# A fused perceiver, attention and expert block: way back and small scores side by side, keys and values in other PSUM banks

## The chip, the cores and the metric

The kernel runs on one NeuronCore of a Trainium2 chip. The metric is the device time of one execution, in microseconds. The engines are TensorE (PE), VectorE (DVE), ScalarE (ACT), GpSimd (POOL) and SyncE (SP, which issues the transfers here). Each takes its instructions in the order in which the program gives them, and semaphores tie the engines to each other.

## What is computed

The input is x, 64 sequences of 32 tokens with 256 features, and a context of 257 rows of 192 features for each sequence. Three residual blocks follow each other, each behind a layer norm:

```python
x = x + xattn(layernorm(x), context)   # top-32 cross attention, FiLM, state-space layer, FFN
x = x + attn(layernorm(x))             # softmax attention, 256 wide within 32 tokens
x = x + ffn(layernorm(x))              # 8 experts, top 2 by router and centroids
```

In xattn, four heads of queries score the 257 context rows, keep 32 each, and their mean weights give a context vector c_t. From it come scale and shift ahead of a state-space layer (the film's input half), and scale and shift behind it (the output half): `y = s4d(x_in); y = y * (1 + g * scale_out) + g * shift_out; xt = x_text + y`. Then come a layer norm, a GELU network of 1024, and another norm. The state-space layer is a convolution over 32 tokens, here as a transform of real matrices: a matmul forward, a product with the kernel's transform, and a matmul back ("the way back"). In attn, `scores = Q @ K.T / 4`, `out = softmax(scores) @ V`, followed by an output projection. In ffn each expert is `gelu(x @ w1 + b1) @ w2 + b2`, summed with the gates. Everything is in float32.

## The kernel before

The 2048 tokens are 16 tiles of 128 rows (four sequences each). The kernel is a software pipeline of four stages: in step n (n = 1 to 18) each engine works for tile a = n (cross attention: scores and top 32), b = n - 1 (context, film, state-space layer, first network), c = n - 2 (its end, then small attention) and dd = n - 3 (experts). A tile out of 0 to 15 is None and its work is left out, so a is None from step 16, and dd is there from step 3. `following` is a's next tile. Every engine's part of a step is a hand-written order in its function `step`; semaphores count what is done, and `wait(engine, semaphore, value)` stands ahead of the instruction that needs it.

PSUM has eight banks of 512 columns: S[0], S[1] (scores of a), B0, B1, PA, C0, D0, D1. An expert's output k goes to half a bank, to D1 for k = 0, 1, 4, 5 and to D0 for k = 2, 3, 6, 7.

The part of a step that the change touches, on PE in its order (L numbers are the lines of the kernel before):

- scores_end(a, 1): the last matmuls of a's scores (L1187, L1190).
- experts 0 and 1 of dd (L1257), into D1.
- The way back of b (L1355): for each of four sequences a matmul of 96 contracted rows to 32 output rows, 256 columns, into B0's upper half. It waits for both halves of had (L970, L973 on DVE) and for `qk_a`, the copies of the folded queries.
- transposes of xl2 of c (L1145) into C0's lower half.
- The film's output half of b (L1362, L1363): 512 columns into B1.
- Keys of c (L1368, the product of query and key weights with xT2) into C0's upper half, values (L1370) into C0's lower half. They wait for xT2_a.
- experts 2 and 3 (L1257), into D0, behind g2b_a, the experts' second gelu.
- Small scores of c (L1380): eight matmuls to 32 output rows and 32 columns, into C0.
- query of the tile after following (L1152), into PA's upper half.
- experts 4 to 7 (L1257). Experts 4 wait until DVE has taken outputs 0 and 1 (`acc_v`), experts 6 until it has taken 2 and 3.
- The output of small attention (L1406), 32 matmuls, behind pT_blk; transposes of hn (L1145); expert bias (L1255); output projection (L1417); the first network (L1240), and in the next step its second half (L1263).

On ACT: gelus of dd (L634, helper `gelus`), the copies of the folded queries (L650, `keyed`), exps(a, 1) (L671, two Exp), copy of xT2 (L629, helper `copy`, as all copies with a semaphore), of the way back's result to yb (L629, semaphore y_a), of keys (L720) and values (L629, v_a), Exp of the small scores (p_c, L723), copy of the query. A table load (ACT_TABLE_LOAD) stands wherever the next function is in another table.

On DVE: maxima and take (L810, L817) of a's second half, gated(0, 1) (L883, L885: takes expert outputs out of PSUM times their gates), take8 (L837), then y times scale and plus shift (L986, L989), xt (L995), its statistics (L1000, L1001) with a find8 (L831, maximum search) between them, gated 2 (L889), the row maximum of the small scores (L1008), gated 3 (L889), the row weights of the softmax (L1013 to L1015), hn (L1018, behind POOL's root `rs0_g`), pT_blk (L1021), gated 4 and 5. The softmax weights pT_blk are the transposed weights spread over four blocks.

## Time and profile before

| | us |
|---|---|
| median of 3 runs | 589.39 (585.61 to 591.86) |
| the profiled execution | 583.03 |
| its span, first to last instruction | 581.2 |
| PE, DVE busy in it | 540.8, 481.4 |
| ACT, POOL busy in it | 295.5, 287.3 |

The profile is one execution. A row of a timeline gives the start in us from the span's start, the time from the first start to the last end, engine, line, operation, what is written from what, the shape, and how many. In brackets stands idle time before it, and what ended it. PEld is the loading of weights. Most matmuls in float32 appear as two records. The names are those of buffers: PC is PA and C0, BB is B0 and B1, D is D0 and D1, and ang is the large buffer that most of the small tiles share.

### The profile page before, as it was taken

The numbers are of one execution on the slowest core, as the hardware profiler recorded it, in microseconds if no ns is written. First come the engines' busy times: TensorE is split into PE (matmuls) and PEld (weight loads), VectorE is DVE, ScalarE is ACT, GpSimd is POOL, SyncE is SP. The second block draws the span as 40 slices with busy tenths as digits, with TensorE's granted clock in tenths as the row PEclk, the third lists the DMA queues.
The fourth block names the chain that finished last, engine by engine and source line by source line (L and its number), as shares of the span: only waits on it lengthen the run. The fifth ranks groups of instructions, "written<-read, shape, count | busy, mean of one in ns | idle before, by whom it ended". The sixth has DMA issues, their size and how long they took to land.

```text
span 581.2 us, 13157 instructions
## 1 busy us (share of the span) xinstructions
PE 540.8 (93%) x4580; PEld 401.6 (69%) x4580; DVE 481.4 (83%) x1748; ACT 295.5 (51%) x770; POOL 287.3 (49%) x669
## 2 busy tenths in 40 slices
PE   2868878999999999999999999999999999998986
PEld 1425454868686877778686868687877868685854
DVE  7898786789998989889898989898988989885444
ACT  3131443374746555564737474746555564645533
POOL 5972155626445375636363635546272636262521
PEclk9998988999999999999999999999999999999999
DMA  8972412030403040220303040404030120000000
GB/s 190 339 293 99 197 42 83 2 117 2 136 1 136 1 124 13 68 70 21 114 20 117 3 135 0 136 1 134 3 114 23 54 73 11 1 11 1 11 1 18
DMA packets 17957, 42.33 MB, mean 73 GB/s; under 512 B 2770, under 2 KB 9570, under 8 KB 17380
## 3 DMA queue, kind: packets, MB, share of 16 engines
q1 hardware_dynamic: 17892, 41.51, 21.3%
q8 instruction: 36, 0.59, 0.4%
q14 instruction: 29, 0.24, 0.1%
HBM read 39.37 MB, written 2.13 MB: 71 GB/s over the span
## 4 chain that ended last, share of the span: by engine, by line
PE 80%; DVE 10%; POOL 2%; issue 2%; ACT 2%; DMA 1%; SPq 1%; DVEq 0%; ACTq 0%; POOLq 0%
PE D L1240 10%; PE BB L1240 9%; PE BB L1263 9%; PE D L1257 8%; PE SS L1181 5%; PE SS L1187 3%; PE BB L1228 3%; PE BB L1229 3%; PE PC L1417 2%; PE BB L1363 2%; PE BB L1362 2%; PE PC L1368 2%; PE PC L1213 2%; PE PC L1370 2%; PE PC L1406 2%
## 5 line engine op out<-in xcount | busy, mean ns | idle before, releaser
L551 POOL TENSOR_SCALAR var_in<-mv 128x1 f32<-128x1 f32 x64 | 14.5, 226 | 203.8 <-DVE mv L1001 116.1
L837 DVE MATCH_REPLACE8 work<-top,work 128x257 f32<-128x257 f32 x192 | 77.6, 410 | 0.0
L831 DVE MAX8 top<-work 128x8 f32<-128x257 f32 x192 | 73.1, 415 | 0.0
L1240 PE MATMUL D<-ang,e_w 128*128 128x128 f32 x512 | 69.7, 281 | 0.0
L1240 PEld LDWEIGHTS D<-ang,e_w 128*128 128x128 f32 x512 | 61.6, 192 | 10.0 <-issue 10.0
L1257 PE MATMUL D<-expw,ang 128*128 128x256 f32 x256 | 65.7, 389 | 1.8 <-ACT ang L634 1.8
L1240 PEld LDWEIGHTS BB<-ang,w 128*128 128x128 f32 x512 | 59.6, 192 | 1.9 <-ACT ang L734 1.1
L1240 PE MATMUL BB<-ang,w 128*128 128x128 f32 x512 | 59.9, 276 | 0.9 <-ACT ang L734 0.9
L634 ACT ACTIVATE ang<-BB,cols 128x128 f32<-128x128 f32 x128 | 36.5, 368 | 47.0 <-PE BB L1240 47.0
L1263 PE MATMUL BB<-expw,ang 128*128 128x256 f32 x256 | 57.9, 380 | 0.0
L1257 PEld LDWEIGHTS D<-expw,ang 128*128 128x128 f32 x256 | 45.8, 190 | 12.9 <-issue 4.5
L1263 PEld LDWEIGHTS BB<-expw,ang 128*128 128x128 f32 x256 | 47.5, 191 | 5.7
L889 DVE SCALAR_TENSOR_TENSOR ang<-D,gate,ang 128x256 f32<-128x256 f32 x96 | 43.1, 477 | 6.0 <-PE D L1257 4.1
L671 ACT ACTIVATE expo<-SS,nmax,srs 128x257 f32<-128x257 f32 x64 | 32.7, 561 | 18.2 <-DVE work L817 17.8
L1181 PE MATMUL SS<-ctx_t,qk 128*128 128x257 f32 x128 | 35.5, 402 | 3.9 <-DMA mask_t<-mask_scratch 2.7
L553 POOL TENSOR_TENSOR rstd<-var_in,mhalf 128x1 f32<-128x1 f32 x64 | 36.5, 570 | 5.3
L671 ACT ACT_TABLE_LOAD x28 | 35.9, 1283 | 0.5
L634 ACT ACTIVATE ang<-D,cols 128x128 f32<-128x128 f32 x128 | 35.7, 355 | 0.2
L1181 PEld LDWEIGHTS SS<-ctx_t,qk 128*128 128x128 f32 x128 | 23.5, 202 | 12.8 <-issue 9.5
L584 POOL TENSOR_SCALAR wsel<-head,rsum_row,tm_tile 128x32 f32<-128x32 f32 x64 | 29.4, 471 | 3.8 <-issue 1.2
L629 ACT ACTIVATE ang<-D 128x256 f32<-128x256 f32 x16 | 6.1, 383 | 43.3 <-PE D L1145 43.3
L810 DVE MAX8 top<-SS 128x8 f32<-128x257 f32 x64 | 24.2, 418 | 4.2 <-PE SS L1190 4.2
(279 smaller groups left out, 1253.4 us busy)
## 6 DMA issues: line engine op xcount, KB each, us to landing
ctx_n<-in_ctx_n SPq DMA_DIRECT2D x16, 768.0 KB, 4.4
ctx_t<-in_ctxT SPq DMA_DIRECT2D x16, 514.0 KB
ctx_t<-in_ctxT SPq DMA_DIRECT2D x16, 257.0 KB
xT<-in_xT SPq DMA_DIRECT2D x16, 128.0 KB, 2.8
x_all<-in_x SPq DMA_DIRECT2D x4, 512.0 KB, 11.3
out<-out_sb SPq DMA_DIRECT2D x16, 128.0 KB, 1.7
ctx_l<-in_ctx_l SPq DMA_DIRECT2D x16, 96.0 KB, 5.1
w<-in_W SPq DMA_DIRECT2D x1, 1024.0 KB
```

What stands on the lines that cost most here:

```text
L553: link(tt(rstd[k][:, 0:1], w, mhalf[:, 0:1], ALU.pow))
L584: nc.gpsimd.tensor_scalar(wsel[:, k, :], sel[:, :], rsum_row[:, k:k + 1], tm_tile[:, k:k + 1], ALU.mult, ALU.mult).then_inc(s["wsel_g"], 1)
L634: ins = A(dst[:, k, :], bank[:, 128 * (k % 4):128 * (k % 4) + 128], ACT.Gelu, bias=bias[:, k:k + 1])
L671: A(expo[:, 2 * q + k, :], S[k][:, 0:G], ACT.Exp, bias=nmax[:, 2 * q + k:2 * q + k + 1], scale=srs[:, a.n, 2 * q + k:2 * q + k + 1]).then_ ...
L810: V.max(top[:, 2 * q + k, 0:8], S[k][:, 0:G]).then_inc(chains["top"], 1)
L831: V.max(top[:, 2 * q + k, 8 * r8:8 * r8 + 8], work[:, 2 * q + k, :]).then_inc(chains["top"], 1)
L837: V.match_replace(work[:, 2 * q + k, :], top[:, 2 * q + k, 8 * r8:8 * r8 + 8], work[:, 2 * q + k, :], TAKEN).then_inc(chains["taken"], 1)
L889: V.scalar_tensor_tensor(acc[k % 2][:, :], bank, gate[:, k:k + 1], acc[k % 2][:, :], ALU.mult, ALU.add).then_inc(s["acc_v"], 1)
L1181: MM(S[u][:, 0:G], qk1[a.p][:, 2 * q + u, :, :].rearrange("p h t -> p (h t)"), ctx_t1[a.p][:, 2 * q + u, :], start=True, stop=False)
L1240: ins = MM(bank[:, 128 * m:128 * m + 128], w[:, k, at:at + 128], xs[:, 128 * k:128 * k + 128], start=k == 0, stop=k == 1)
L1257: MM(bank, act2[:, k, :], e_w2[:, k, :], start=True, stop=True).then_inc(s["eo_mm"], 1)
L1263: ins = MM(B1[:, 0:D], act1[:, k, :], w2[:, k, :], start=k == 0, stop=k == HID // 128 - 1)
```

## The change

It holds in steps where tiles b and dd both exist (`joined(b, dd)`, steps 3 to 16). Elsewhere the old order stays.

PE: the transposes of xl2 go ahead of experts 0 and 1 and into D0, with a wait for g2b_a. After experts 0 and 1 come the keys (into D0's upper half), the film's output half, the way back, the small scores (into C0 as before), the values (now into PA's lower half), experts 2 and 3, and the query, which has a new wait until the values are copied.

ACT: the copy of xT2 and of the keys go ahead of exps(a, 1), each from D0, the keys behind a semaphore of their own (key_mm); the copy of the values goes behind the Exp of the small scores and comes from PA.

DVE: both find8 and the row maximum go ahead of the y multiply; the row weights go ahead of gated 2; pT_blk goes behind gated 3 and ahead of hn.

The diff, cut to its core (the helper functions repeat the old instructions):

```diff
+        def joined(b, dd):
+
+            return bool(b and dd)
...
+            def columns(c, bank):
+
+                wait(act, s["xT2_mm"], c.count(1, 1))
+                copy(xT2[:, :], bank[:, 0:D], "xT2_a")
+
+            def keys(c, bank):
+
+                wait(act, s["key_mm"], c.count(1, 1))
+                copy(xmT[:, :], bank[:, D:2 * D], "v_a")
+
+            def values(c, bank):
+
+                wait(act, s["v_mm"], c.count(1, 1))
+                copy(v_c[:, :], bank[:, 0:D], "v_a")
...
...
                     gelus(act2, 1, D0, e_b1, "e1b_mm", "g2b_a", dd)
                 if following:
                     keyed(following)
+                if joined(b, dd):
+                    columns(c, D0)
+                    keys(c, D0)
                 if a:
                     exps(a, 1)
-                if c:
-                    wait(act, s["xT2_mm"], one(c))
-                    copy(xT2[:, :], C0[:, 0:D], "xT2_a")
+                if c and not joined(b, dd):
+                    columns(c, C0)
                 if c and c.n == NT - 1:
                     A(ahead[:, :], b1[:, 0:1], ACT.Exp)
                 if b:
                     wait(act, s["inv_mm"], one(b))
                     copy(yb[:, :], B0[:, D:2 * D], "y_a")
-                if c:
+                if c and not joined(b, dd):
                     wait(act, s["v_mm"], one(c))
-                    A(xmT[:, :], C0[:, D:2 * D], ACT.Copy)
-                    copy(v_c[:, :], C0[:, 0:D], "v_a")
+                    keys(c, C0)
+                    values(c, C0)
+                if c:
                     wait(act, s["nmaxc_v"], one(c))
                     A(p_c[:, :], C0[:, D:D + T], ACT.Exp, bias=nmax_c[:, :], accum_out=sum_c[:, :]).then_inc(s["pc_a"], 1)
+                if joined(b, dd):
+                    values(c, PA)
                 if next_tile(following):
                     query(next_tile(following))
...
+            def row_maximum(c):
+
+                wait(dve, s["s_mm"], c.count(1, 1))
+                V.reduce_max(nmax_c[:, :], C0[:, D:D + T], AXX, negate=True).then_inc(s["nmaxc_v"], 1)
+
+            def row_weights(c):
+
+                wait(dve, s["pc_a"], c.count(1, 1))
+                link(V.reciprocal(rsum_c[:, :], sum_c[:, :]))
+                link(V.tensor_scalar(pn_c[:, :], p_c[:, :], rsum_c[:, :], None, ALU.mult))
+                V.transpose(pT_c[:, :], pn_c[:, :]).then_inc(chains["pT"], 1)
+
+            def weight_blocks(c):
+
+                wait(dve, chains["pT"], c.count(1, 1))
+                V.tensor_tensor(pT_blk[:, :, :], pT_c[:, :].rearrange("p (o t) -> p o t", o=1).broadcast_to([128, BT, T]), block_mask[:, :, :], ALU.mult).then_inc(s["pt_v"], 1)
...
...
                     gated(range(0, 2))
                 if a:
                     take8(a, 0, 2, (1,))
+                if joined(b, dd):
+                    if a:
+                        find8(a, 0, 3)
+                    row_maximum(c)
                 if b:
                     wait(dve, s["y_a"], one(b))
                     wait(dve, s["y_mm"], one(b))
...
                 if b:
                     wait(dve, chains["y"], b.count(2, 1))
                     V.tensor_tensor(yb[:, :], yb[:, :], B1[:, D:2 * D], ALU.add).then_inc(chains["y"], 1)
-                if a:
...
-                if a:
+                if a and not joined(b, dd):
...
...
                     V.bn_aggr(mv[0][:, :], bn[0][:, :]).then_inc(s["st0_v"], 1)
                 if a and a.n == 1:
                     tokens(4, 8)
+                if joined(b, dd):
+                    row_weights(c)
                 if dd:
                     gated((2,))
-                if c:
-                    wait(dve, s["s_mm"], one(c))
-                    V.reduce_max(nmax_c[:, :], C0[:, D:D + T], AXX, negate=True).then_inc(s["nmaxc_v"], 1)
+                if c and not joined(b, dd):
+                    row_maximum(c)
                 if dd:
                     gated((3,))
                 if c:
-                    wait(dve, s["pc_a"], one(c))
-                    link(V.reciprocal(rsum_c[:, :], sum_c[:, :]))
-                    link(V.tensor_scalar(pn_c[:, :], p_c[:, :], rsum_c[:, :], None, ALU.mult))
-                    V.transpose(pT_c[:, :], pn_c[:, :]).then_inc(chains["pT"], 1)
+                    if joined(b, dd):
+                        weight_blocks(c)
+                    else:
+                        row_weights(c)
                 if b:
                     wait(dve, s["rs0_g"], one(b))
                     V.tensor_scalar(hn[:, :], xt[:, :], mv[0][:, 0:1], rstd[0][:, 0:1], ALU.subtract, ALU.mult).then_inc(s["hn_v"], 1)
-                if c:
-                    wait(dve, chains["pT"], one(c))
-                    V.tensor_tensor(pT_blk[:, :, :], pT_c[:, :].rearrange("p (o t) -> p o t", o=1).broadcast_to([128, BT, T]), block_mask[:, :, :], ALU.mult).then_inc(s["pt_v"], 1)
+                if c and not joined(b, dd):
+                    weight_blocks(c)
                 if dd:
...
+                def film_out():
+
+                    MM(B1[:, :], zT1[:, :], film1[:, 512:1024], start=True, stop=False)
+                    MM(B1[:, :], zT2[:, :], film2[:, 512:1024], start=False, stop=True).then_inc(s["y_mm"], 1)
...
+                def keys_values(keys, values):
+
+                    wait(pe, s["xT2_a"], one(c))
+                    if keys is not None:
+                        for m in range(2):
+                            for k in range(2):
+                                ins = MM(keys[:, D + 128 * m:D + 128 * m + 128], qk_w[:, k, 128 * m:128 * m + 128], xT2[:, 128 * k:128 * k + 128], start=k == 0, stop=k == 1)
+                        ins.then_inc(s["key_mm"], 1)
+                    if values is not None:
+                        for k in range(2):
+                            ins = MM(values[:, 0:D], xT2[:, 128 * k:128 * k + 128], wv_w[:, k, :], start=k == 0, stop=k == 1)
+                        ins.then_inc(s["v_mm"], 1)
+
+                def small_scores():
+
+                    wait(pe, s["v_a"], c.count(2, 1 if joined(b, dd) else 2))
+                    wait(pe, s["x2_v"], c.count(1, 0))
+                    for k in range(BT):
+                        rows = slice(T * k, T * k + T)
+                        for m in range(2):
+                            cols = slice(128 * m + T * k, 128 * m + T * k + T)
+                            ins = MM(C0[rows, D:D + T], xmT[:, cols], xT2[:, cols], start=m == 0, stop=m == 1)
+                    ins.then_inc(s["s_mm"], 1)
...
                     scores(a, 1)
                 if a:
                     scores_end(a, 1)
+                if joined(b, dd):
+                    wait(pe, s["xl2_v"], one(c))
+                    wait(pe, s["g2b_a"], one(dd))
+                    if dd.n == 0:
+                        pe.wait_ge(s["route_a"], 1)
+                    transposes(D0, xl2, "xT2_mm")
                 if dd:
                     experts(range(0, 2))
-                if b:
-
-                    wait(pe, s["had_v"], b.count(2, 2))
-                    if following:
-                        wait(pe, s["qk_a"], following.count(2, 2))
-                    if b.n == 0:
-                        pe.wait_ge(s["ld_w"], LD_W)
-                    for k in range(BT):
-                        ins = MM(B0[T * k:T * k + T, D:2 * D], dft_y[:, :], had[0:NF, k, :], start=True, stop=True)
-                    ins.then_inc(s["inv_mm"], 1)
-                if c:
-                    wait(pe, s["xl2_v"], one(c))
-                    wait(pe, s["x2_v"], c.count(1, 0))
-                    transposes(C0, xl2, "xT2_mm")
-                if b:
-                    MM(B1[:, :], zT1[:, :], film1[:, 512:1024], start=True, stop=False)
-                    MM(B1[:, :], zT2[:, :], film2[:, 512:1024], start=False, stop=True).then_inc(s["y_mm"], 1)
-                if c:
-                    wait(pe, s["xT2_a"], one(c))
-                    for m in range(2):
-                        for k in range(2):
-                            ins = MM(C0[:, D + 128 * m:D + 128 * m + 128], qk_w[:, k, 128 * m:128 * m + 128], xT2[:, 128 * k:128 * k + 128], start=k == 0, stop=k == 1)
-                    for k in range(2):
-                        ins = MM(C0[:, 0:D], xT2[:, 128 * k:128 * k + 128], wv_w[:, k, :], start=k == 0, stop=k == 1)
-                    ins.then_inc(s["v_mm"], 1)
+                if joined(b, dd):
+                    keys_values(D0, None)
+                    free_banks()
+                    film_out()
+                    way_back()
+                    small_scores()
+                    keys_values(None, PA)
+                elif b:
+                    free_banks()
+                    way_back()
+                    if c:
+                        columns(C0)
+                    film_out()
+                elif c:
+                    columns(C0)
+                if c and not joined(b, dd):
+                    keys_values(C0, C0)
                 if dd:
                     experts(range(2, 4))
-                if c:
-                    wait(pe, s["v_a"], one(c))
-                    for k in range(BT):
-                        rows = slice(T * k, T * k + T)
-                        for m in range(2):
-                            cols = slice(128 * m + T * k, 128 * m + T * k + T)
-                            ins = MM(C0[rows, D:D + T], xmT[:, cols], xT2[:, cols], start=m == 0, stop=m == 1)
-                    ins.then_inc(s["s_mm"], 1)
+                if c and not joined(b, dd):
+                    small_scores()
                 if next_tile(following):
                     if dd:
                         wait(pe, s["gT_a"], one(dd))
+                    if joined(b, dd):
+                        wait(pe, s["v_a"], c.count(2, 2))
                     query(next_tile(following))
                 if a and a.n == 1:
                     wait(pe, s["mr1_v"], following.count(4, 0))
...
                 if c:
 
                     wait(pe, s["pt_v"], one(c))
+                    wait(pe, s["v_a"], c.count(2, 2))
```

## Rows read from the trace of the kernel before

**Rows 1.** The page's totals by engine: busy us, share of the span, instructions.

```profile
PE 540.8 (93%) x4580; PEld 401.6 (69%) x4580; DVE 481.4 (83%) x1748; ACT 295.5 (51%) x770; POOL 287.3 (49%) x669
```

**Rows 2.** Busy us (instructions) of PE, PEld, DVE, ACT, POOL; clock, DMA, GB/s; L1406 one step earlier.

```profile
311.00:342.00 31.00, 30.99 (x277) 23.75 (x273) 27.40 (x105) 17.82 (x47) 15.47 (x37) 1.00 0.18 59
...
290.23 0.65 PE L1406 MATMUL PC<-ang,pT_blk 128*32 128x64 f32 x32
```

**Rows 3.** PE in order of time, one step: start us, us, what, out<-in, shape.

```profile
312.34 1.13 PE L1257 MATMUL D<-expw,ang 128*128 128x256 f32 x4
313.40 0.64 PE L1355 MATMUL BB<-had,dft_y 96*32 96x256 f32 x8
313.97 0.44 PE L1145 MATMUL PC<-head,ang 128*128 128x128 f32 x2
314.24 1.02 PE L1362 MATMUL BB<-film,zT 128*128 128x512 f32 x2
...
315.96 1.05 PE L1368 MATMUL PC<-ang,qk_w 128*128 128x128 f32 x8
316.86 1.03 PE L1370 MATMUL PC<-wvo,ang 128*128 128x256 f32 x4
317.72 1.03 PE L1257 MATMUL D<-expw,ang 128*128 128x256 f32 x4
318.68 0.35 PE L1380 MATMUL PC<-ang 128*32 128x32 f32 x16
318.96 0.71 PE L1152 MATMUL PC<-xT,head 128*128 128x128 f32 x4
319.51 1.89 PE L1257 MATMUL D<-expw,ang 128*128 128x256 f32 x8
321.41 0.65 PE L1406 MATMUL PC<-ang,pT_blk 128*32 128x64 f32 x32
```

**Rows 4.** ACT in order of time, the same step; in brackets idle time before.

```profile
309.82 1.09 ACT L634 ACTIVATE ang<-D,cols 128x128 f32<-128x128 f32 x4
...
312.56 0.55 ACT L650 ACTIVATE qk<-BB 128x256 f32<-128x256 f32 x2 [0.24 <-DVE had L970]
313.13 1.28 ACT L671 ACT_TABLE_LOAD   x1
...
315.61 0.39 ACT L629 ACTIVATE ang<-BB 128x256 f32<-128x256 f32 x1
...
319.40 0.29 ACT L723 ACTIVATE p_c<-PC,nmax_c 128x32 f32<-128x32 f32 x1 [0.82 <-DVE nmax_c L1008]
```

**Rows 5.** DVE in order of time, the same step.

```profile
315.56 0.41 DVE L837 MATCH_REPLACE8 work<-top,work 128x257 f32<-128x257 f32 x1
316.24 0.42 DVE L986 TENSOR_TENSOR ang<-ang,BB 128x256 f32<-128x256 f32 x1 [0.26 <-PE BB L1363]
...
317.69 0.42 DVE L831 MAX8 top<-work 128x8 f32<-128x257 f32 x1
318.03 0.41 DVE L1000 BATCH_NORM_STATS2 bn<-ang 128x6 f32<-128x256 f32 x1
318.47 0.18 DVE L1001 BATCH_NORM_AGGREGATE mv<-bn 128x2 f32<-128x6 f32 x1
...
319.19 0.18 DVE L1008 TENSOR_REDUCE nmax_c<-PC 128x1 f32<-128x32 f32 x1
319.29 0.48 DVE L889 SCALAR_TENSOR_TENSOR ang<-D,gate,ang 128x256 f32<-128x256 f32 x1
319.81 0.16 DVE L1013 RECIPROCAL rsum_c<-sum_c 128x1 f32<-128x1 f32 x1
...
320.74 0.41 DVE L1018 TENSOR_SCALAR ang<-ang,mv,rstd 128x256 f32<-128x256 f32 x1 [0.21 <-POOL rstd L413]
321.07 0.28 DVE L1021 TENSOR_TENSOR pT_blk<-pT_c,cols 128x128 f32<-128x128 f32 x1
```

**Rows 6.** ACT in step 16, the table load ahead of p_c.

```profile
534.95 1.28 ACT L723 ACT_TABLE_LOAD   x1
```

More of the change, by code:

```diff
@@ L717, in step @@
                     copy(yb[:, :], B0[:, D:2 * D], "y_a")
+                if c and not joined(b, dd):
+                    wait(act, s["v_mm"], one(c))
+                    keys(c, C0)
+                    values(c, C0)
                 if c:
[L719 to L721 removed]
                     wait(act, s["nmaxc_v"], one(c))
                     A(p_c[:, :], C0[:, D:D + T], ACT.Exp, bias=nmax_c[:, :], accum_out=sum_c[:, :]).then_inc(s["pc_a"], 1)
+                if joined(b, dd):
+                    values(c, PA)
                 if next_tile(following):
@@ L995, in step @@
                     V.tensor_tensor(xt[:, :], yb[:, :], xln[b.n % 3][:, :], ALU.add).then_inc(s["xt_v"], 1)
-                if a:
+                if a and not joined(b, dd):
                     find8(a, 0, 3, (1,))
@@ L1257, in experts, with free_banks, way_back, columns @@
                             MM(bank, act2[:, k, :], e_w2[:, k, :], start=True, stop=True).then_inc(s["eo_mm"], 1)
+                def free_banks():
+                    wait(pe, s["had_v"], b.count(2, 2))
+                    if following:
+                        wait(pe, s["qk_a"], following.count(2, 2))
+                def way_back():
+                    if b.n == 0:
+                        pe.wait_ge(s["ld_w"], LD_W)
+                    for k in range(BT):
+                        ins = MM(B0[T * k:T * k + T, D:2 * D], dft_y[:, :], had[0:NF, k, :], start=True, stop=True)
+                    ins.then_inc(s["inv_mm"], 1)
+                def film_out():
+                    MM(B1[:, :], zT1[:, :], film1[:, 512:1024], start=True, stop=False)
+                    MM(B1[:, :], zT2[:, :], film2[:, 512:1024], start=False, stop=True).then_inc(s["y_mm"], 1)
+                def columns(bank):
+                    wait(pe, s["xl2_v"], one(c))
+                    wait(pe, s["x2_v"], c.count(1, 0))
+                    transposes(bank, xl2, "xT2_mm")
+                def keys_values(keys, values):
[11 more added lines that the diff above has]
+                    wait(pe, s["v_a"], c.count(2, 1 if joined(b, dd) else 2))
+                    wait(pe, s["x2_v"], c.count(1, 0))
+                    for k in range(BT):
+                        rows = slice(T * k, T * k + T)
[3 more added lines that the diff above has]
+                    ins.then_inc(s["s_mm"], 1)
                 def down(half):
```

4 lines of the change are left out of this document (2 added, 2 removed).

## The prediction

> **What bounds the kernel now.** I read the totals by engine first: TensorE (PE) is busy for 93% of the span, VectorE (DVE) for 83%, ScalarE (ACT) for half [rows 1]. An average of that sort hides the stages, so the table by stretches came next: in a stretch of 31 us in the middle PE is busy for 30.99 us at granted clock 1.00 and DVE for 27.40 [rows 2]. One step of the pipeline takes 31.18 us (two starts of L1406, 290.23 and 321.41) [rows 2, 3]. I therefore follow one step, from 312.3 to 322 us, in order of time on each engine.
>
> PE goes from block to block without a gap. A block's price is the distance to the next block's start [rows 3]: experts 0 and 1 1.06 us, the way back 0.57, the transposes of xl2 0.27, the film's output half 1.72 (two weights), keys 0.90, values 0.86, experts 2 and 3 0.96, small scores 0.28, query 0.55, experts 4 to 7 1.90. Some are dearer than their streaming. Two query matmuls with 128 columns are a quarter of the film's streaming (0.43), but cost 0.55 behind the small scores; experts 2 and 3 cost 0.10 more than the values, which are of the same shape. The extra stands where 32-column blocks (way back, small scores) meet full ones.
>
> The second thing to see is how near DVE is. It waits 0.26 us for the film's output (L986), and from there it works almost without pause to pT_blk, ready at 321.07 + 0.28 = 321.35 [rows 5]. L1406, which waits for pT_blk, starts at 321.41 [rows 3]. PE and DVE are both late there to within some 0.1 us. ACT has room: its y copy (L629, 315.61) is done at 316.00 [rows 4], before DVE takes it.
>
> **The change part by part.** It holds for steps that have b and dd, n = 3 to 16: 13 with tile a (3 to 15), and step 16 without.
>
> *PE's order.* New: transposes (to D0), experts 0 and 1, keys (to D0), film, way back, small scores, values (to PA), experts 2 and 3, query, experts 4 to 7. No matmul is added or dropped. Two 32-column blocks with full ones around each become one, so one of two entries and one of two exits goes. Bare streaming of the blocks from 312.34 to 319.51, by the film's 1.72 for 1024 columns, is 3584 columns (experts 1024, film 1024, keys 512, values 512, query 256, the way back's four parallel outputs as 256) or 6.02 us, with 0.22 for the transposes and about 0.2 for the small scores 6.4; the blocks take 7.17 [rows 3]. Of the 0.7 left over at most about half goes (0.35); adding block by block with the extras where full and 32-column blocks still meet gives 0.16. I take 0.3. Below nothing it can't go, since the new order has fewer changes of width. Experts 4 would start at 319.2.
>
> *Wait for g2b_a ahead of the transposes.* D0 is still read by the second gelus, which end at 309.82 + 1.09 = 310.91 [rows 4]; PE is there at 312.34. Nothing, with 1.4 us of cover.
>
> *Keys, and ACT behind them.* This is where I expect the price. ACT takes instructions in order, and its copies of xT2 and keys now stand ahead of the exponentials exps(a, 1). ACT ends keyed at 312.56 + 0.55 = 313.11 and copies xT2 till 313.51 (0.38 us a copy). PE: transposes from 312.34, experts 0 and 1 till about 313.5, keys from 313.6, whose last result is there 1.05 later [rows 3], at 314.65. ACT stands idle from 313.51, copies the keys till 315.05, and only then runs the table load for Exp, which ran at 313.13 before. Nor can the load be hoisted: in step 16 it stands at 534.95, behind two copies, with Exp's use after it, though ACT had been idle [rows 6]. From the load's start to the y copy's end it was 316.00 - 313.13 = 2.87 [rows 4]; now y_a comes at 315.07 + 2.87 - 0.27 (the xT2 copy that stood between is gone) = 317.7, which is 1.7 later than before.
>
> At this place a rule can be weighed. The rows show the load at 1.28 us and the next Exp work at once behind it, in 2.87 for the load, two exponentials and two copies [rows 4]. The Trainium skill (ScalarE: Activation LUTs, "What ACT_TABLE_LOAD costs") puts a drain of about 1.38 us on top of the load. By that y_a would be 1.38 later still and the whole some 18 us dearer; the rows of this case have no room for it, and I give it no chance of its own.
>
> *DVE.* It ends L837 at 315.97, fills 0.75 with two maxima (0.42 each, overlapping), and then waits for the small scores [rows 5]. PE: film from 314.5 to 316.2, way back to about 316.75, small scores to 316.95, last result (0.35 after their start) at about 317.15. Row maximum 317.2 to 317.38. Then y waits for y_a till 317.73. What follows has no filler left: multiply, add, xt, bn_stats, bn_aggr at the 0.44 that L1000 to L1001 shows for a dependent pair, so aggr starts at 317.73 + 4 x 0.44 = 319.49 and ends at 319.67 (before: 318.65). Row weights (three operations, L1013 to L1015) take 320.74 - 0.21 - 319.81 = 0.72 and now stand ahead of gated 2 and 3. They run from 319.60 (an operation starts some 0.08 before the one before has ended) to 320.3; their input p_c needs 0.41 from row maximum or y copy [rows 4, 5], so it is there at 318.1. Gated 2 and 3 take 0.40 + 0.48: from 320.24 to 321.12 (before: 319.77).
>
> *The wait that takes the place.* Experts 6 and 7 write D0, where 2 and 3 stand, and so wait for acc_v of gated 3. PE arrives there at 319.2 + 0.87 = 320.1 and waits till 321.17 (0.05 behind DVE, as at L1406): 1.1 us. Queued behind are L1406 and the rest of the step. Experts 6 and 7 with the entry to 32 columns take 0.96: L1406 starts at 322.13, against 321.41. **+0.72 us a step.** PE's 0.3 saved only lengthens this wait. pT_blk comes at 321.4, no longer late: the wait that the change could take away is worth at most 0.1.
>
> *After it.* The normalization's root on POOL stays 320.74 - 318.65 = 2.09 long, so hn starts at 321.8 and is ready at 322.2, before the transposes at 322.7. DVE comes out 0.8 later, PE 0.72, and everything to the step's end follows PE as before.
>
> *Values to PA, and query's wait for them.* PE ends values at about 317.9, ACT copies them by 318.5; PE, with experts 2 and 3 between, reaches the query at 318.8. Nothing, with 0.3 of cover. Without the cover it would only eat into the 1.1 of the wait behind.
>
> *Step 16.* There is no a, so ACT has no exponentials. The load for p_c (534.95) runs over a microsecond earlier, since the value copies no longer stand ahead of it, while y comes later, behind film and way back, by about 0.6. Experts 6 and 7 have the same new wait. One against the other, between -1 and +0.7 us once; I take nothing [rows 6].
>
> **The sum.** 13 x 0.72 = 9.4 us. On the profiled execution, 583.03 us with a span of 581.2, that is 592.4. That execution is 1.1% below the median of the runs shown, 589.39; on the median it gives 598.8.
>
> **Rivals.**
> - *y is not late.* If the exponentials' work got out of y's way (a table load that overlaps the wait for the keys), y would follow the row maximum at 317.38, 0.35 earlier: +0.37 a step, +4.8 us, 594.2. For it: ACT idles 1.1 us ahead of the keys. Against: rows 6. Chance 0.17.
> - *DVE is in time (not slower).* Should the dependent chain run so tight that gated 3 ends by 320.05, PE's saving comes through: 0.3 and the 0.1 at L1406, 13 x 0.4 = 5.2 us, 584.2. The point is 320.1 at experts 6; DVE would have to be 1.1 us faster than worked out. For it: PE is the busiest engine, and L1406 really waits on DVE. Against: even with y at once behind the row maximum gated 3 ends at 320.8. Chance 0.1.
> - *DVE carries its delay on.* DVE leaves the place 0.1 later than PE; if links cost 0.3 more in the row weights and y (no filler between them), the wait grows to 1.4, +1.02 a step, +13.3 us, 602.7. For it: five dependent operations now stand bare. Chance 0.13.
> - My forecast: 0.6.
>
> **Numbers.** A measurement of this kernel tells about 1% from no change. Slower by over 1% (above 595.3): my case nearly whole, the carried delay, part of the first rival: 0.69. Within 1%: most of the first rival and much of the second: 0.23. Faster by over 1%: 0.08, if the second gives a little more than worked out. The range takes the first rival and the third, with about 2 us to the side for the spread of runs: 588 to 604.
>
> **What the profile would show.** Right: L1257 for experts 6 and 7 with PE idle 0.8 to 1.3 us before it, released by DVE L889; ACT idle about 1.1 us before the key copy and the table load some 1.9 us later in the step; DVE idle about 0.5 before the row maximum and 0.35 before the y multiply; 31.9 us from one L1406 to the next. Wrong: no idle time before experts 6, or a period at or below 31.18, or the table load standing ahead of the key copy.

## The result and the profile after

The changed kernel takes 599.39 us (median of 4 runs, 596.42 to 601.25), against 588.21 us for the kernel before (4 runs, 585.61 to 591.86). The ratio is 1.0205, with a 95% interval of 1.0148 to 1.0261: the change is slower, by 1.5 to 2.6%, and whether by more than 2% these runs don't tell. The forecast was 598.8. Some executions of these kernels run longer at a lower granted clock, and the ratios in this document leave them out.

The profiled execution took 598.03 us, with a span of 596.2 us. Its totals by engine (they answer to [rows 1]):

```profile
PE 545.3 (91%) x4580; PEld 402.9 (68%) x4580; DVE 481.7 (81%) x1748; ACT 296.6 (50%) x770; POOL 287.8 (48%) x669
```

No engine works noticeably more than before: PE 545.3 us against 540.8, DVE 481.7 against 481.4. What grew is the time in which PE has nothing to do. The span is 15.0 us longer than that of the kernel before, and the starts of the small attention's output (L1406, now L1495) divide it. Over the 13 steps 3 to 15 its start moves by 417.77 us (104.37 to 522.14), against 406.55 (101.42 to 507.97): **11.2 us, 0.86 a step**. The period of a step in the middle is 32.06 us against 31.18. Steps 16 and 17 give 0.1, the tail 0.7, and 2.95 lie ahead of step 3, where nothing was changed. The stretch from 50 to 60 us shows what goes with it (table by stretches, columns as in [rows 2]), first for the kernel before:

```profile
50.00:60.00 10.00, 8.73 (x177) 5.62 (x177) 7.62 (x19) 1.23 (x4) 0.00 (x0) 0.87 0.55 202
```

and for the changed kernel:

```profile
50.00:60.00 10.00, 9.54 (x126) 5.12 (x130) 7.28 (x19) 0.28 (x1) 0.00 (x0) 0.53 0.57 215
```

The granted clock of this stretch is 0.87 of full speed in one and 0.53 in the other. That is not the work of the change, since ahead of step 3 nothing differs: in the profiles of the ten kernels below it lies between 0.50 (three) and 1.00 (four), and the latter reach the first output some 5 us or more before the former. From here on I compare periods of a step. In each profile but those of e4 and e10 they repeat within 0.02 us from 260 to 480 us (in e4 within 0.05, and one period of e10 is 0.06 shorter). One earlier step, from about 230 us on, takes some 0.9 us more in every kernel, the one before included.

PE in one step after the change, in order of time, columns as in [rows 3]:

```profile
320.58 0.44 PE L1190 MATMUL D<-head,ang 128*128 128x128 f32 x2
...
324.50 0.64 PE L1315 MATMUL BB<-had,dft_y 96*32 96x256 f32 x8
324.96 0.34 PE L1350 MATMUL PC<-ang 128*32 128x32 f32 x16
325.23 1.13 PE L1339 MATMUL PC<-wvo,ang 128*128 128x256 f32 x4
...
327.50 1.03 PE L1302 MATMUL D<-expw,ang 128*128 128x256 f32 x4
329.31 1.13 PE L1302 MATMUL D<-expw,ang 128*128 128x256 f32 x4 [0.77 <-DVE ang L930]
330.37 0.65 PE L1495 MATMUL PC<-ang,pT_blk 128*32 128x64 f32 x32
330.95 0.44 PE L1190 MATMUL BB<-head,ang 128*128 128x128 f32 x2
331.32 0.70 PE L1300 MATMUL D<-e_b,gateT 128*128 128x256 f32 x2
331.86 1.03 PE L1506 MATMUL PC<-wvo,ang 128*128 128x256 f32 x4
```

The step's first block starts at 320.58 where it was 312.34, so 8.24 is to be taken off to compare with [rows 3]. Up to experts 4 PE needs 6.92 us (320.58 to 327.50), against 7.17 (312.34 to 319.51): the new order does save 0.25. The way back takes 0.46 until the small scores start, and these 0.27; ahead of the way back the film's second half costs 0.95 (323.55 to 324.50), where it was 0.86 (315.10 to 315.96). Then experts 6 and 7 (L1302 at 329.31) wait for DVE's L930, gated 3. From experts 4 to L1495 it is 2.87 us instead of 1.90. A second loss stands behind it: from L1495 to the output projection (L1506) it is 1.49 instead of 1.32, since the transposes are followed by the bias expert only after 0.37, not 0.28, and this by the projection after 0.54, not 0.46. From there to the next step's start, 20.78 against 20.79, nothing differs. Three terms and this rest so make the period: 6.92 + 2.87 + 1.49 + 20.78 = 32.06.

ACT in the same step, answering to [rows 4]:

```profile
321.25 0.39 ACT L633 ACTIVATE ang<-D 128x256 f32<-128x256 f32 x1
322.89 0.38 ACT L633 ACTIVATE ang<-D 128x256 f32<-128x256 f32 x1 [1.25 <-PE D L1335]
323.29 1.28 ACT L690 ACT_TABLE_LOAD   x1
324.58 1.02 ACT L690 ACTIVATE expo<-SS,nmax,srs 128x257 f32<-128x257 f32 x2
325.50 0.38 ACT L633 ACTIVATE ang<-BB 128x256 f32<-128x256 f32 x1
```

The xT2 copy at 321.25, 1.25 us of waiting for the keys, their copy, and only then the table load at 323.29. The y copy ends at 325.88, or 317.64 on the old clock; it was 316.00.

DVE, answering to [rows 5]:

```profile
325.38 0.19 DVE L891 TENSOR_REDUCE nmax_c<-PC 128x1 f32<-128x32 f32 x1 [0.50 <-PE PC L1350]
325.91 0.42 DVE L1031 TENSOR_TENSOR ang<-ang,BB 128x256 f32<-128x256 f32 x1 [0.34 <-ACT ang L633]
...
327.74 0.18 DVE L1046 BATCH_NORM_AGGREGATE mv<-bn 128x2 f32<-128x6 f32 x1
327.84 0.13 DVE L896 RECIPROCAL rsum_c<-sum_c 128x1 f32<-128x1 f32 x1
...
328.42 0.83 DVE L930 SCALAR_TENSOR_TENSOR ang<-D,gate,ang 128x256 f32<-128x256 f32 x2
329.17 0.28 DVE L903 TENSOR_TENSOR pT_blk<-pT_c,cols 128x128 f32<-128x128 f32 x1
330.07 0.41 DVE L1064 TENSOR_SCALAR ang<-ang,mv,rstd 128x256 f32<-128x256 f32 x1 [0.62 <-POOL rstd L417]
330.40 0.87 DVE L930 SCALAR_TENSOR_TENSOR ang<-D,gate,ang 128x256 f32<-128x256 f32 x2
```

It waits 0.50 for the small scores and 0.34 for y's copy, then works without fillers to the end of gated 3 (329.25), on which experts 6 start 0.06 later. hn waits 0.62 for POOL's root, and gated 4 and 5 behind it end at 331.27; the bias expert starts at 331.32.

### The profile page after: what moved, and what is told of

Its sections match the earlier page's. It is cut to its first block, busy times and chain, and to the rows that moved or that the text cites. A ratio compares the mean times of both kernels' runs of the same rounds, so it can differ in the third digit from the quotient of the medians.

```text
span 596.2 us, 13190 instructions
## 1 busy us (share of the span) xinstructions
PE 545.3 (91%) x4580; PEld 402.9 (68%) x4580; DVE 481.7 (81%) x1748; ACT 296.6 (50%) x770; POOL 287.8 (48%) x669
## 3 DMA queue, kind: packets, MB, share of 16 engines
HBM read 39.37 MB, written 2.13 MB: 70 GB/s over the span
## 4 chain that ended last, share of the span: by engine, by line
PE 69%; DVE 16%; ACT 8%; issue 3%; POOL 2%; DMA 1%; SPq 1%; DVEq 0%; ACTq 0%; POOLq 0%
PE D L1285 9%; PE BB L1285 9%; PE BB L1357 9%; PE D L1302 6%; PE SS L1226 5%; PE SS L1232 3%; ACT L690 3%; PE BB L1273 3%; PE BB L1274 2%; PE PC L1506 2%; ACT expo L690 2%; PE D L1335 2%; DVE ang L930 2%; PE PC L1258 2%; PE BB L1428 2%
## 5 line engine op out<-in xcount | busy, mean ns | idle before, releaser
L1302 PE MATMUL D<-expw,ang 128*128 128x256 f32 x256 | 67.2, 387 | 13.6 <-DVE ang L930 11.9
L855 DVE MAX8 top<-work 128x8 f32<-128x257 f32 x192 | 71.8, 415 | 0.0
L1302 PEld LDWEIGHTS D<-expw,ang 128*128 128x128 f32 x256 | 45.1, 190 | 25.1 <-DVE ang L930 17.9
L633 ACT ACTIVATE ang<-D 128x256 f32<-128x256 f32 x44 | 17.0, 386 | 63.1 <-PE D L1190 45.4
L930 DVE SCALAR_TENSOR_TENSOR ang<-D,gate,ang 128x256 f32<-128x256 f32 x96 | 41.3, 471 | 3.7 <-PE D L1302 3.6
L690 ACT ACT_TABLE_LOAD x28 | 35.9, 1283 | 0.5
```

The costliest lines, as they stand in the source:

```text
L690: A(expo[:, 2 * q + k, :], S[k][:, 0:G], ACT.Exp, bias=nmax[:, 2 * q + k:2 * q + k + 1], scale=srs[:, a.n, 2 * q + k:2 * q + k + 1]).then_ ...
L855: V.max(top[:, 2 * q + k, 8 * r8:8 * r8 + 8], work[:, 2 * q + k, :]).then_inc(chains["top"], 1)
L930: V.scalar_tensor_tensor(acc[k % 2][:, :], bank, gate[:, k:k + 1], acc[k % 2][:, :], ALU.mult, ALU.add).then_inc(s["acc_v"], 1)
L1302: MM(bank, act2[:, k, :], e_w2[:, k, :], start=True, stop=True).then_inc(s["eo_mm"], 1)
```

## The experiments

Line numbers shift by a few lines from kernel to kernel. The table gathers the three terms of the period that differ for all of them but e4; "to experts 4" runs from the step's first block in this stretch, "to output" on to the small attention's output, "to projection" on to the output projection, in us. The ratio is to the kernel before, timed on the same chips.

| kernel | to experts 4 | to output | to projection | period | ratio (95%) |
|---|---|---|---|---|---|
| before | 7.17 | 1.90 | 1.32 | 31.18 | 1 |
| changed | 6.92 | 2.87 | 1.49 | 32.06 | 1.0205 (1.0148 to 1.0261) |
| e1 row weights behind gated 3 | 6.92 | 2.31 | 2.13 | 32.15 | 1.0227 (1.0147 to 1.0308) |
| e2 table load early | 6.92 | 2.58 | 1.49 | 31.78 | 1.0135 (1.0061 to 1.0209) |
| e3 gated 4 ahead of hn | 6.92 | 2.87 | 1.29 | 31.86 | 1.0139 (1.0040 to 1.0239) |
| e6 = e2 + e3 | 6.92 | 2.58 | 1.29 | 31.57 | 1.0081 (1.0034 to 1.0128) |
| e5 = e1 + e2 + e3 | 6.92 | 2.02 | 1.74 | 31.47 | 1.0079 (1.0037 to 1.0121) |
| e8 one more operation on DVE | 6.92 | 3.18 | 1.30 | 32.19 | 1.0231 (1.0112 to 1.0349) |
| e7 film last | 7.18 | 2.00 | 1.77 | 31.72 | 1.0103 (1.0030 to 1.0176) |
| e9 = e5, bias expert first | 6.92 | 2.02 | 1.40 | 31.42 | 1.0036 (0.9993 to 1.0080) |
| e10 = e5, y narrow | 6.92 | 1.82 | 1.43 | 30.96 | 0.9952 (0.9913 to 0.9992) |

**e1: the row weights back behind gated 2 and 3.** My theory (T) was one late DVE chain that meets PE twice, at experts 6 and at the bias expert. The rival (S) was that the wait at experts 6, the only place I had priced in the prediction, is everything.

```diff
-                if joined(b, dd):
-                    row_weights(c)
                 if dd:
                     gated((2,))
...
                 if c:
+                    row_weights(c)
                     if joined(b, dd):
                         weight_blocks(c)
-                    else:
-                        row_weights(c)
```

> The changed kernel with the row weights (three DVE operations, 0.7 us) back behind gated 2 and 3. Theory T: the price is one DVE chain from the late y copy, and it meets PE twice, at experts 6 (gated 3) and right behind at the bias expert (hn, then gated 4 and 5). Taking the first away leaves the second: the idle time before experts 6 falls from 0.77 to about 0.1, but the bias expert still starts where it did, so the period of a step stays within 0.15 us of 32.06, and the time within 2 us of the changed kernel's. Rival S: the wait at experts 6 is all of the price; the period falls by 0.6 to 0.7 us, to about 31.4, and the time by 8 to 9 us.

Period 32.15, which is 0.09 longer. PE in one step:

```profile
331.07 1.13 PE L1299 MATMUL D<-expw,ang 128*128 128x256 f32 x4 [0.22 <-DVE ang L930]
332.13 0.65 PE L1492 MATMUL PC<-ang,pT_blk 128*32 128x64 f32 x32
332.94 0.44 PE L1187 MATMUL BB<-head,ang 128*128 128x128 f32 x2 [0.16 <-DVE ang L1061]
333.73 0.70 PE L1297 MATMUL D<-e_b,gateT 128*128 128x256 f32 x2 [0.35 <-DVE ang L930]
```

The wait before experts 6 has shrunk from 0.77 to 0.22, and L1492 starts 0.56 earlier in the step. All of it comes back behind: the transposes wait for hn (0.16), the bias expert for gated 4 and 5 (0.35), and "to projection" grows from 1.49 to 2.13. The 0.09 on top comes from POOL: one operation of the root that hn waits for (L416) takes 0.48 us here, from 331.59 on, where it took 0.40 in the changed kernel. DVE's pT_blk (331.64 to 331.93) now runs beside it, and hn comes 0.09 later in the step. Rival S falls: 0.56 us taken from the largest wait on the busiest engine bought nothing, as the next waits hang on the same late chain.

**e2: the table load early.** A one-column Exp between the two copies of ACT lets the load run while ACT waits for the keys.

```diff
                     columns(c, D0)
+                    if a:
+                        A(ahead[:, :], b1[:, 0:1], ACT.Exp)
                     keys(c, D0)
```

> The changed kernel with a one-column Exp on ACT between the copies of xT2 and of the keys, so that the table load runs while ACT waits for the keys. Theory T: the load costs by making y late; y's multiply then starts right behind the row maximum, 0.35 us earlier in the step, and everything behind follows: period 31.7, 4.5 us less. Rival L: the small scores' place (row maximum) sets DVE's chain anyway, and y's copy is not what counts: period unchanged at 32.06.

Period 31.78, 0.28 less; 0.35 was expected. ACT, then DVE:

```profile
323.11 1.28 ACT L730 ACT_TABLE_LOAD   x1
...
324.51 0.37 ACT L633 ACTIVATE ang<-D 128x256 f32<-128x256 f32 x1
...
326.66 0.38 ACT L633 ACTIVATE ang<-BB 128x256 f32<-128x256 f32 x1 [0.86 <-PE BB L1317]
```

```profile
326.84 0.19 DVE L893 TENSOR_REDUCE nmax_c<-PC 128x1 f32<-128x32 f32 x1 [0.50 <-PE PC L1352]
327.08 0.42 DVE L1033 TENSOR_TENSOR ang<-ang,BB 128x256 f32<-128x256 f32 x1
```

The load stands at 323.11, right behind xT2's copy, and ends at 324.39, about when the keys' last result is there (324.30). The one-column Exp behind it makes the copy of the keys 0.16 later in the step than in the changed kernel (2.47 us into it instead of 2.31), which the film covers here. The exponentials are done in time, and the y copy now waits only for the way back. On DVE L1033 follows the row maximum in 0.24 us instead of 0.53, that is, 0.29 earlier. Rival L falls. The rest of the 0.35 isn't to be had, because y's copy waits for the way back and ends only at 327.04.

**e3: gated 4 ahead of hn.**

```diff
+                if joined(b, dd):
+                    gated((4,))
                 if b:
                     wait(dve, s["rs0_g"], one(b))
...
                 if dd:
-                    gated(range(4, 6))
+                    gated(range(5 if joined(b, dd) else 4, 6))
```

> The changed kernel with gated 4 ahead of hn on DVE, in the 0.62 us in which DVE waits for POOL's root. Theory T: the wait at the bias expert goes (about 0.1 to 0.17 us a step), period 31.9 to 31.95, 1.5 to 2 us less. Rival S: nothing, 32.06.

Period 31.86, 0.20 less, a little more than the 0.1 to 0.17 expected.

```profile
328.43 1.13 PE L1304 MATMUL D<-expw,ang 128*128 128x256 f32 x4 [0.78 <-DVE ang L930]
329.49 0.65 PE L1497 MATMUL PC<-ang,pT_blk 128*32 128x64 f32 x32
330.07 0.44 PE L1192 MATMUL BB<-head,ang 128*128 128x128 f32 x2
330.35 0.60 PE L1302 MATMUL D<-e_b,gateT 128*128 128x256 f32 x2
```

The wait before experts 6 is as it was (0.78), but from the transposes to the bias expert it is 0.28 again. "To projection" falls to 1.29: the second loss is gone, and it was this one.

**e4 and e8: the same operation more on DVE, in the kernel before and in the changed one.** Which engine sets the pace is shown by lengthening the other.

```diff
+                if b and dd:
+                    V.bn_stats(spare[:, :], x_all[:, b.n, :])
                 if dd:
                     gated((2,))
```

> The kernel before with one bn_stats of 0.33 to 0.41 us more on DVE, into a spare tile, ahead of gated 2 in steps with b and dd. Theory T: DVE is co-critical there (pT_blk is late by up to 0.1), so L1406 starts 0.3 us later in each of 13 steps: period 31.5, 4 us more. Rival P: PE alone bounds the kernel before and DVE has slack; period 31.18, no change.

The ratio is 0.9946 (0.9885 to 1.0007): no slower, where T had 4 us more. The granted clock of its profiled execution was 0.95 of full speed from 100 us on, so its period doesn't compare; DVE does, by its own rows. First gated 2 in the kernel before, then e4:

```profile
318.79 0.48 DVE L889 SCALAR_TENSOR_TENSOR ang<-D,gate,ang 128x256 f32<-128x256 f32 x1
```

```profile
322.95 0.42 DVE L987 TENSOR_TENSOR ang<-ang,BB 128x256 f32<-128x256 f32 x1 [0.37 <-PE BB L1366]
...
325.29 0.40 DVE L1006 BATCH_NORM_STATS2 spare<-x_all 128x6 f32<-128x256 f32 x1
325.60 0.47 DVE L890 SCALAR_TENSOR_TENSOR ang<-D,gate,ang 128x256 f32<-128x256 f32 x1
...
327.48 0.41 DVE L1021 TENSOR_SCALAR ang<-ang,mv,rstd 128x256 f32<-128x256 f32 x1
327.80 0.28 DVE L1024 TENSOR_TENSOR pT_blk<-pT_c,cols 128x128 f32<-128x128 f32 x1
```

From the y multiply to the end of pT_blk it is 5.13 us (322.95 to 328.08). It was 5.11 without the operation [rows 5]. The operation went into two gaps. In the kernel before, DVE ended bn_aggr at 318.65 and started gated 2 at 318.79, when PE was done with experts 2 and 3 (317.72 + 1.03 = 318.75); from the start of bn_aggr to that of gated 2 it is 0.32 there and 0.41 here, though the new operation stands between them. The remaining 0.09 come off the wait for POOL's root ahead of hn (0.22 from the transpose's end to hn there, 0.13 here). Rival P has the outcome: PE bounds the kernel before, and DVE could take a third of a microsecond more without any loss.

In the changed kernel (the operation stands ahead of the row weights):

> The changed kernel with one bn_stats (0.33 us) more on DVE ahead of the row weights, the same operation that the kernel before took without any loss. Theory T: here DVE's chain sets experts 6, so L1495 (output of small attention) starts 0.33 us later in the step and the period is 32.3 to 32.4, 3 to 4 us more. Rival P: PE bounds as in the kernel before, period 32.06.

```profile
325.02 1.13 PE L1304 MATMUL D<-expw,ang 128*128 128x256 f32 x4 [1.10 <-DVE ang L931]
326.08 0.65 PE L1497 MATMUL PC<-ang,pT_blk 128*32 128x64 f32 x32
...
326.94 0.60 PE L1302 MATMUL D<-e_b,gateT 128*128 128x256 f32 x2
```

The idle time before experts 6 grows from 0.77 to 1.10, and "to output" from 2.87 to 3.18: here DVE sets it. But the period grows by 0.13 alone, to 32.19, not by the 0.24 to 0.34 expected. Since PE now reaches the transposes later, gated 5 is done in time, and "to projection" falls from 1.49 to 1.30. Two waits on one chain don't add; the later one lives on what the earlier leaves. That is e1 in reverse.

**e6 and e5: edits together.** e6 is e2 and e3; e5 is e6 and the edit of e1.

> The changed kernel with both the early table load and gated 4 ahead of hn. Theory T: the two prices stand at different places (y late; bias expert late), so they add: 0.28 and 0.20 us off 32.06, period 31.6, 6 us less than the changed kernel. Rival O: they overlap, period 31.75 or more.

Period 31.57: 0.49 off 32.06, where 0.28 and 0.20 make 0.48. They add. The first meets the chain at its head, the second its end.

> As the run before, and the row weights back behind gated 2 and 3. Alone that edit gave nothing, since hn and gated 4 and 5 were late behind it. Theory T: with those two out of the way it now pays; experts 6 don't wait, hn is what PE waits for, period 31.35 (0.25 less than the run before). Rival R: the row weights' place never matters, period as in the run before, 31.6.

Period 31.47, 0.10 less than e6; 0.25 was expected. The direction of T holds (alone the edit cost 0.09), the size doesn't:

```profile
319.74 2.09 PE L1303 MATMUL D<-expw,ang 128*128 128x256 f32 x8
321.76 0.65 PE L1496 MATMUL PC<-ang,pT_blk 128*32 128x64 f32 x32
322.58 0.44 PE L1191 MATMUL BB<-head,ang 128*128 128x128 f32 x2 [0.16 <-DVE ang L1065]
```

Experts 4 to 7 run through in 2.02 us with no idle time shown, but the transposes wait 0.16 for hn, and "to projection" is 1.74. hn hangs on y by way of four bare DVE operations and POOL's root, and neither edit shortens these. The edit even lengthens the root: as in e1, its L416 takes 0.49 us beside pT_blk (0.40 in e6), and hn comes 0.09 later in the step than in e6. That is over half of the 0.15 by which I missed.

**e7: the film last.** The order keys, way back, small scores, film; p_c ahead of the exponentials on ACT; row maximum and row weights ahead of y on DVE; with e2 and e3. Of the edit, the part in PE's order:

```diff
                     free_banks()
-                    film_out()
                     way_back()
                     small_scores()
+                    film_out()
                     keys_values(None, PA)
```

> A candidate to be no slower than the kernel before: way back and small scores still side by side, but ahead of the film's output half; p_c ahead of exps(a, 1) on ACT, row maximum and row weights ahead of the y multiply on DVE, early table load, gated 4 ahead of hn. Theory T: the price of the change was what stood on DVE behind y; with the softmax's operations moved into the wait for y, gated 3 is in time and PE keeps its 0.25 us: period 31.1 to 31.3, within 1% of the kernel before. Rival X: the transposes to D0 and ACT's wait for the keys cost by themselves; period 31.6 or more.

Period 31.72, ratio 1.0103: a miss.

```profile
323.09 0.64 PE L1324 MATMUL BB<-had,dft_y 96*32 96x256 f32 x8
323.79 0.35 PE L1359 MATMUL PC<-ang 128*32 128x32 f32 x16
324.07 1.12 PE L1329 MATMUL BB<-film,zT 128*128 128x512 f32 x2
```

"To output" is 2.00, as hoped. But the small scores stand 0.70 behind the way back where it was 0.46, because they wait for ACT's copy of the keys (323.37 to 323.73), which the film had hidden. 0.16 of that lateness is the early table load's (see e2). "To experts 4" is 7.18, so the whole saving of the new order is lost, and the film, now last, makes y late again (5.28 us into the step; in e2 it was 5.04). It isn't alone in this: y's copy ends at 326.03 and DVE's own searches at 326.19, where the film's last result is there at 326.06. The number is the rival's (31.6 or more), the cause only in part: the wait for the keys' copy does cost here, but it is PE that waits, where nothing covers it any more, and y is late by another way.

**e9: the bias expert ahead of the transposes.** e5 with gated 4 and 5 both ahead of hn, and on PE experts(8), the bias expert, ahead of the transposes of hn (the part on PE is shown).

```diff
+                if joined(b, dd):
+                    experts(range(8, NE + 1))
                 if b:
                     wait(pe, s["hn_v"], one(b))
                     wait(pe, s["xt_v"], one(b))
                     transposes(B0, hn, "hT_mm")
```

> The kernel with three edits (e5: early table load, row weights behind gated 2 and 3, gated 4 ahead of hn), and now gated 4 and 5 ahead of hn, and on PE the expert bias ahead of the transposes of hn, so that PE has work while hn is late. Theory T: of e5's period of 31.47, 0.3 to 0.35 us stand between the output of small attention and the output projection (1.74 us against 1.32 before); they go, period 31.1 to 31.2, equal to the kernel before within what can be measured. Rival H: hn comes later by the gated operation ahead of it and nothing is gained, 31.45.

Period 31.42; 31.1 to 31.2 was expected, and 31.45 by the rival.

```profile
320.90 0.65 PE L1496 MATMUL PC<-ang,pT_blk 128*32 128x64 f32 x32
...
322.08 0.38 PE L1191 MATMUL BB<-head,ang 128*128 128x128 f32 x2
322.30 1.03 PE L1509 MATMUL PC<-wvo,ang 128*128 128x256 f32 x4
323.36 1.83 PE L1286 MATMUL BB<-ang,w 128*128 128x128 f32 x14
```

"To projection" did fall from 1.74 to 1.40, as expected. But then L1286, the first network, starts 1.06 us behind the projection, against 0.87 in the kernel before: it needs hT, the copy of the transposes. These now stand behind the bias expert and start 1.18 us behind L1496 (0.58 in the kernel before). hn is ready at 321.81 and no longer what they wait for, so the rival's reason, a later hn, doesn't hold, though its number does. Behind this wait the block also takes 0.11 us more (3.68 to L1358, against 3.57 in the kernel before), and what follows the projection to the step's end, 20.77 to 20.79 us in the other kernels of the table, is 21.08 here. The wait has moved one block on. Still, this is the best full version, 0.36% above the kernel before, which its interval doesn't tell from it. None beats the kernel before.

**e10: what PE's new order is worth with DVE in time.** e5 with the y multiply and add on 32 of 256 columns; the other columns of tile b leave out the film's output scale and shift.

```diff
-                    V.tensor_tensor(yb[:, :], yb[:, :], B1[:, 0:D], ALU.mult).then_inc(chains["y"], 1)
+                    V.tensor_tensor(yb[:, 0:32], yb[:, 0:32], B1[:, 0:32], ALU.mult).then_inc(chains["y"], 1)
```

> What the new order of PE is worth by itself. As e5, but the y multiply and add work on 32 of the 256 columns in every step, so the other columns leave out the film's output scale and shift: some 0.5 us off DVE's chain behind y. Theory T: nothing on DVE is late any more; PE's part up to experts 4 stays at 6.92 us (7.17 before), experts 4 to the output of small attention fall to 1.90 and from there to the output projection to 1.32, as before; period 30.93, 0.25 less than the kernel before. Rival N: the new order gives PE nothing; period 31.18 or more.

```profile
322.86 0.19 DVE L1033 TENSOR_TENSOR ang<-ang,BB 128x32 f32<-128x32 f32 x1
...
323.30 0.42 DVE L1042 TENSOR_TENSOR ang<-ang,xln 128x256 f32<-128x256 f32 x1
```

The chain is 0.47 us shorter (0.22 from each to the next instead of 0.45), and the period is 30.96, within 0.03 of what was expected and 0.22 under the kernel before. Rival N falls. Its terms were off by a tenth each, in opposite directions: "to output" is 1.82, less than the kernel before ever had (1.90), and "to projection" 1.43 instead of 1.32, since the bias expert still starts just as gated 5 ends. With DVE all but in time the change would have been worth 13 x 0.22 = 2.9 us, half a per cent, and the measured ratio of 0.9952 agrees. One thing is left untested: the kernel before has y at full width. 0.08 of the 0.22 stand at "to output", where a shorter DVE chain might have helped the old order too, and no run narrows y there.

## Why the prediction was right

The mechanism and its place were right, and most of the steps to within a few hundredths. For the comparison 8.24 us are taken off the changed kernel's times:

- *PE's order*: 0.3 saved until experts 4 (start at 319.2). Measured 0.25, start at 327.50 - 8.24 = 319.26; e10 confirms it as time that PE gives back if nothing behind is late.
- *Keys, and ACT behind them*: y_a at 317.7 was forecast, 317.64 measured; e2 shows that 0.28 of each step's loss hangs on it. The load wasn't hoisted, as [rows 6] had said.
- *DVE*: the y multiply at 317.73 against 317.67, gated 3 done at 321.12 against 329.25 - 8.24 = 321.01.
- *The wait that takes the place*: L1406 at 322.13 was forecast, and L1495 started at 330.37 - 8.24 = 322.13. Two small errors cancel here: gated 3 was 0.1 earlier, and experts 6 and 7 took 1.06 to the next block, not 0.96. e8 shows that DVE sets this place. Of the signs that I had named, the idle time before experts 6 came out at 0.77, just under the 0.8 to 1.3, as part of the loss stands in the block behind the wait and not in idle time; the other signs were there (period 32.06 against 31.9).
- *After it*: the step that was mis-sized. I wrote that everything to the step's end follows PE as before. It didn't: "to projection" grew by 0.17 us, 0.72 became 0.88 in the middle of the run, and 9.4 us became 11.2. I had hn right (321.8; measured 330.07 - 8.24 = 321.83), but I never set gated 4 and 5 behind it (end at 323.03) against the bias expert's start (322.13 + 0.86 = 322.99, were it not late). e3 shows that 0.20 hung on just this.
- *Values to PA, step 16*: no wait stands before the query; L1495 of step 16 follows by 29.90 against 29.93. Both nothing, as said.

My claim on the kernel before, that DVE and PE are both late at L1406 by some 0.1, was half right. "To output" was 1.90 there and is 1.82 in e10, where pT_blk comes early, so L1406 did wait 0.08 us for it, unseen among the idle times. But what followed from it in e4, that DVE's chain grows by what is added, was wrong: the chain had gaps (waits for experts 2 and 3 and for POOL's root) that took the operation in. It cost the forecast nothing, since I had priced the place at 0.1 at most.

As for the rivals: "y is not late" describes e2, which a dummy Exp makes true: 0.28 a step off, not 0.35. "DVE is in time" describes e10 and is worth 0.22 a step, not 0.4. "DVE carries its delay on" did happen in a mild form (0.17, of the 0.3 named), though at the bias expert and not in the row weights. That the total came out within 0.6 us (599.39 against 598.8) is partly luck. I had 9.4 us for the change on a base of 589.39; measured were 11.2 on a base of 588.21. The error of the change, 1.8 us, and that of the base, 1.2, point in opposite directions.

What stays open is whether hn could be made earlier. What holds it is y, four dependent DVE operations and POOL's root (330.07 - 327.92 = 2.15 us from the end of bn_aggr to hn). A version that shortens this was not tried, beyond e10, which leaves work out to get there.

## What to carry to other kernels

Ahead of a reordering that saves the busiest engine some tenths, walk the slower engine's chain from the moved result to every later point where the busiest one waits for it, not only to the first: here the first wait cost most, but taking it away alone (e1) gave nothing. A copy moved ahead of a function that needs another table moves the table load too; a small call of that function, placed where the engine idles anyway, takes the load off the path (here it cost the next copy 0.16 us, which was covered in e2 and not in e7). When a change puts two blocks side by side, look at what the block between them had been hiding (here the key copy, the row weights and y's copy), for that is what it uncovers.

## What was not expected of the hardware

- A PE block that starts on a semaphore costs some 0.1 us more than the same block without a wait, on top of the wait: experts 6 and 7 took 1.06 to the next block against the 0.96 of the same shapes, 0.54 against 0.46 for the bias expert. The rows of the weight loads (PEld) show where it stands. For experts 4, whose matmuls start at 327.50, the load starts 0.10 earlier, at 327.40; for experts 6 load and matmuls start together, at 329.31. In the rows of PE's idle time this isn't seen, as PE counts as busy. So a wait that has only just ended still costs (e5: 2.02 us to the output without idle time shown, where e10 has 1.82 for the same matmuls).
- The table load took 1.28 us, and the copy and exponentials stood against it on both sides: in e2 the load starts 0.02 us behind a copy, and in the changed kernel the first exponential starts 1.29 behind the load's start. The Trainium skill (ScalarE: Activation LUTs, "What ACT_TABLE_LOAD costs") has the 1283 ns, and a drain of about 1380 ns beside it. The first agrees with this trace, the second doesn't show: by an estimate from it, y's copy would have come 1.4 us later than it did.
- The price of passing from full blocks to 32-column blocks and back can be read block by block. Experts 2 and 3, ahead of 32-column blocks, cost 0.96 in the kernel before, and 0.86 in the changed one, where a full block follows: an entry costs 0.10. The query behind small scores costs 0.55, and 0.44 where a full block stands ahead of it: an exit costs 0.11. One pair less is thus 0.21 of the 0.25 us that the new order saves up to experts 4. The rest is two terms that nearly cancel: 0.10 less at experts 0 and 1, which no longer stand right behind the scores, and 0.07 more at the keys, which wait for the copy of xT2. The Trainium skill (TensorEngine Tiling (Array Packing), "Key Properties") says that changing the tiling mode drains the array, without a figure; the trace shows a price at these changes, not the drain itself.
- A small POOL operation takes longer beside DVE's pT_blk: L416 of the root takes 0.34 us in e8 and e10, where pT_blk starts over 0.2 us behind its start, 0.40 in the changed kernel, where pT_blk starts 0.1 ahead of it, and 0.48 in e1, where pT_blk starts 0.05 behind its start. That pT_blk is the cause isn't shown by a run of its own.
